# Counting the edges of a graph in windows of twelve nodes: how much of the old counts each window reads back

## The reference, cut to what matters

```python
def _sage_mean(x, src, dst, W_self, W_neigh, b, n_nodes):
    deg = jax.ops.segment_sum(jnp.ones_like(dst, dtype=x.dtype), dst, num_segments=n_nodes)
    agg = jax.ops.segment_sum(x[src], dst, num_segments=n_nodes)
    agg = agg / jnp.maximum(deg, 1.0)[:, None]
    return x @ W_self + agg @ W_neigh + b

h = jax.nn.relu(_sage_mean(x, src, dst, W_self1, W_neigh1, b1, n))
h = _sage_mean(h, src, dst, W_self2, W_neigh2, b2, n)
# ... then a layer with an MLP on every edge, and two more that sum over the same edges
```

## Time and profile before

| | us |
|---|---|
| median of 3 runs | 1679.42 (1676.05 to 1679.87) |
| the profiled execution | 1675.27 |
| its span, first to last instruction | 1673.1 |
| counting, first L1762 to first L853 | 18.36 to 308.12 |

### The profile page before, as it was taken

How to read it: one execution, slowest core, us unless ns; L and a number is a source line. 1 busy time by engine, 2 the same in 40 slices (tenths; PEclk the granted TensorE clock), 3 DMA queues, 4 the chain that set the end, 5 groups by cost and what they waited for, 6 DMA issues and landing times.

```text
span 1673.1 us, 30324 instructions
## 1 busy us (share of the span) xinstructions
PE 1451.8 (87%) x9336; PEld 1032.7 (62%) x9336; DVE 754.3 (45%) x2856; ACT 667.5 (40%) x1243; POOL 763.0 (46%) x806
## 2 busy tenths in 40 slices
PE   4899999999958777888989988998898889877997
PEld 3556666555556566666766766766666667654554
DVE  8799999513333222333243333333432343345445
ACT  6766666410023333443345334433443344331113
POOL 3000000000027777777777777777777777721000
PEclk9999999999978999999999998999899989988999
DMA  2000000020053333333333333333333333300001
GB/s 69 1 1 1 2 2 1 8 61 1 0 147 95 83 81 81 79 89 84 79 85 87 80 82 84 85 82 81 84 88 79 81 86 83 82 21 1 0 1 39
DMA packets 158120, 95.18 MB, mean 57 GB/s; under 512 B 119959, under 2 KB 143422, under 8 KB 158030
## 3 DMA queue, kind: packets, MB, share of 16 engines
q0 software_dynamic: 25024, 51.25, 12.0%
q1 hardware_dynamic: 133006, 42.78, 10.5%
HBM read 87.44 MB, written 6.52 MB: 56 GB/s over the span
## 4 chain that ended last, share of the span: by engine, by line
PE 31%; POOL 13%; DMA 11%; issue 9%; DVE 5%; ACT 1%; DVEq 1%; SPq 1%; POOLq 0%; ACTq 0%
POOL arena L735 13%; DMA arena<-x_w1a,idx 9%; PE ps L1167 6%; PE ps L1052 6%; PE ps L1061 5%; PE ps L1045 4%; PE ps L1041 3%; PE ps L1033 3%; PE ps L1102 2%; PE ps L1151 1%; DVE arena L2049 1%; DVE idx L2016 1%; DVEq L336 1%; DMA x_w1b<-arena 1%; DVE stats L2063 1%
## 5 line engine op out<-in xcount | busy, mean ns | idle before, releaser
L735 POOL DMA_INDIRECT arena<-x_w1a,idx x780 | 737.7, 946 | 713.3 <-issue 674.2
L1478 ACT ACTIVATE arena<-ps 88x512 f32<-88x512 f32 x196 | 116.2, 593 | 480.3 <-PE ps L1033 470.0
L1061 PEld LDWEIGHTS ps<-arena 128*128 128x128 f32 x1568 | 208.6, 196 | 111.5 <-issue 72.8
L2049 DVE TENSOR_TENSOR arena<-ps,bias_b 128x512 f32<-128x512 f32 x196 | 135.5, 691 | 208.0 <-PE ps L1052 208.0
L2044 DVE TENSOR_TENSOR arena<-win_i,late 128x96 f32<-128x96 f32 x196 | 50.8, 259 | 391.8 <-PE ps L1061 378.8
L1041 PE MATMUL ps<-ident_f,arena 128*128 128x128 f32 x784 | 130.1, 290 | 107.3 <-DMA arena<-x_w1a,idx 106.4
L1052 PE MATMUL ps<-w_c,arena 128*128 128x128 f32 x1568 | 222.6, 288 | 0.0
L1303 ACT ACTIVATE adj<-ps 128x300 f32 x392 | 171.0, 451 | 108.3 <-PE ps L800 103.8
L1045 PE MATMUL ps<-arena 88*128 88x512 f32 x392 | 208.0, 612 | 3.1 <-ACT arena L1478 3.1
L1052 PEld LDWEIGHTS ps<-w_c,arena 128*128 128x128 f32 x1568 | 205.9, 205 | 0.3
L1061 PE MATMUL ps<-arena 128*128 128x24 f32 x1568 | 197.9, 264 | 4.9 <-ACT arena L1488 1.4
(11 more groups left out here) (205 smaller groups left out, 1406.7 us busy)
## 6 DMA issues: line engine op xcount, KB each, us to landing
arena<-in_edge_attr SPq DMA_DIRECT2D x196, 128.0 KB, 2.3
arena<-x_w1a,idx POOLq DMA_INDIRECT x782
arena<-x_w1b SPq DMA_DIRECT2D x196, 12.0 KB
x_spill<-arena SPq DMA_DIRECT2D x1, 1600.0 KB, 8.6
x_w1a<-arena SPq DMA_DIRECT2D x6, 256.0 KB, 2.3
x_w1b<-arena SPq DMA_DIRECT2D x6, 256.0 KB, 2.7
arena<-x_spill SPq DMA_DIRECT2D x6, 256.0 KB, 3.4
out_x<-arena SPq DMA_DIRECT2D x3, 512.0 KB
```

The costliest lines, as they stand in the source:

```text
L735: pool.indirect_dma_start(out=z_e[v][:, j * D:(j + 1) * D], out_offset=None, in_=xa_d[:, :], in_offset=bass.IndirectOffsetOnAxis(ap=idx[:, ...
L1061: last = pe.matmul(ps[:, WIN_BANK[v % 2], 0:WIN], msg[:, j * P:(j + 1) * P], oh_e[v][:, j, :], start=(j == 0), stop=(j == J - 1))
L2049: dve.tensor_tensor(msg.rearrange("p (j d) -> p j d", d=D), bank(5, J), over(bias_b, J), ALU.add).then_inc(m_sum[v], 1)
```

## The change

Three things change, and the output stays the same.

The matmul that adds old counts (L800, now L805) reads only the first node of each window, 25 columns, 3200 elements apart, and adds them into PSUM columns 12 apart. The other eleven nodes of a window were never counted before, and ACT overwrites them. Only for the last block of the first front in each round, where the window can reach into columns that the second front has written, all twelve are added: two counts in each round, 14 of 392.

The tests become exact for this: each destination of a half must lie within the window and not above the next half's first node (`highest`, `above`), and in each round the last window that adds only one node must end before the second front's first node (`seam_a`, `seam_b`).

`c1_combine` takes both columns of ones: one operation gives max(degree, 0) and max(degree, 1) into `degrees_x`, for all 25 tiles; `dinv` of the first 20 tiles is computed in one operation after the last round. So L844 reads 386 columns instead of 385.

```diff
-        half_all = arena[:, 11136:11136 + HALVES].bitcast(I32)
-        rel = arena[:, 11528:12312]
+        half_all = arena[:, 11136:11136 + HALVES + 1].bitcast(I32)
+        rel = arena[:, 11532:12316]
+        highest = arena[:, 12320:12320 + HALVES]
+        above = words(2, 3).bitcast(F32)[:, 0:NB * J]
+        degrees_x = arena[:, 13156:13156 + 2 * NT].rearrange("p (k u) -> p k u", u=2)
...
                 pe.wait_ge(adj_written, 8 * i + q + (2 if all_before else 1))
-                pe.matmul(ps[:, bank, 0:NT * WIN_A], ident_h[:, :], adj[:, :, bass.ds(b, WIN_A)],
+                shared = WIN_A if (i % RI, v) == (RI - 1, 2) else 1
+                window = ps[:, bank, 0:NT * WIN_A].rearrange("p (k w) -> p k w", w=WIN_A)
+                pe.matmul(window[:, :, 0:shared], ident_h[:, :], adj[:, :, bass.ds(b, shared)],
                           start=False, stop=True).then_inc(cnt_ready, 1)
...
-                    last = pe.matmul(ps[:, c1_bank(k), 0:3 * D + 1], adj[:, u, k * P:(k + 1) * P], mov_x[:, u, 0:3 * D + 1],
+                    last = pe.matmul(ps[:, c1_bank(k), 0:MOV], adj[:, u, k * P:(k + 1) * P], mov_x[:, u, :],
...
+            own.add(dve.scalar_tensor_tensor(out=highest, in0=half_all[:, 0:HALVES], scalar=WIN_A - 1.0,
+                                             in1=half_all[:, 1:HALVES + 1], op0=ALU.add, op1=ALU.min))
...
-            own.add(dve.tensor_reduce(off[:, 1:2], rel, mybir.AxisListType.X, ALU.max))
+            own.add(dve.tensor_tensor(above.rearrange("p (h j) -> p h j", j=J // 2),
+                                      raw_dst.rearrange("p (h j) -> p h j", j=J // 2), tops, ALU.subtract))
+            own.wait()
+            own.add(dve.tensor_reduce(off[:, 1:2], above, mybir.AxisListType.X, ALU.max))
+            own.wait()
             own.add(dve.tensor_reduce(off[:, 2:3], rel, mybir.AxisListType.X, ALU.min))
...
-                own.add(dve.tensor_scalar(off[:, 1:2], off[:, 1:2], WIN_A - 1.0, None, ALU.subtract))
+                own.add(dve.tensor_tensor(differences[:, 0:ROUNDS], seam_a, seam_b, ALU.subtract))
+                own.wait()
+                own.add(dve.tensor_reduce(off[0:1, 6:7], differences[:, 0:ROUNDS], mybir.AxisListType.X, ALU.max))
+                own.wait()
+                own.add(dve.tensor_scalar(off[0:1, 6:7], off[0:1, 6:7], float(WIN_A), None, ALU.add))
...
                 dve.wait_ge(c1_ready, k + 1)
+                own.add(dve.tensor_tensor(degrees_x[:, k, :], ps[:, b, 3 * D:MOV], win_i[:, 0:2], ALU.max))
                 if k < LATE_TILE:
-                    own.add(dve.tensor_scalar(inv_deg[:, k:k + 1], ps[:, b, 3 * D:3 * D + 1], 1.0, None, ALU.max))
-                    own.add(dve.tensor_scalar(dinv[:, k:k + 1], ps[:, b, 3 * D:3 * D + 1], 1.0, None, ALU.add))
                     own.wait()
-                    own.add(dve.reciprocal(inv_deg[:, k:k + 1], inv_deg[:, k:k + 1]))
+                    own.add(dve.reciprocal(inv_deg[:, k:k + 1], degrees_x[:, k, 1:2]))
...
             dve.wait_ge(c1_deg, 1)
+            own.add(dve.tensor_scalar(dinv[:, 0:LATE_TILE], degrees_x[:, 0:LATE_TILE, 0], 1.0, None, ALU.add))
```

More of the change, by code:

```diff
@@ L1718, in _ @@
             dve.wait_ge(loads[1], 32)
-            firsts = half_all.rearrange("p (h a) -> p h a", a=1).broadcast_to([P, HALVES, J // 2])
+            firsts = half_all[:, 0:HALVES].rearrange("p (h a) -> p h a", a=1).broadcast_to([P, HALVES, J // 2])
+            tops = highest.rearrange("p (h a) -> p h a", a=1).broadcast_to([P, HALVES, J // 2])
+            own.add(dve.scalar_tensor_tensor(out=highest, in0=half_all[:, 0:HALVES], scalar=WIN_A - 1.0,
+                                             in1=half_all[:, 1:HALVES + 1], op0=ALU.add, op1=ALU.min))
             own.add(dve.tensor_tensor(rel.rearrange("p (h j) -> p h j", j=J // 2),
@@ L1753, in in_bounds @@
                 own.add(dve.tensor_scalar(off[0:1, 9:10], off[0:1, 9:10], float(WIN + WIN_A), None, ALU.add))
+                seam_a = base_a.rearrange("p (r m) -> p r m", m=8 * RI)[:, :, 8 * (RI - 1) + 2]
+                seam_b = base_row[0:1, :].rearrange("p (r m) -> p r m", m=RB)[:, :, FB]
+                own.add(dve.tensor_tensor(differences[:, 0:ROUNDS], seam_a, seam_b, ALU.subtract))
[3 more added lines that the diff above has]
+                own.add(dve.tensor_scalar(off[0:1, 6:7], off[0:1, 6:7], float(WIN_A), None, ALU.add))
                 for c in range(EARLY):
@@ L2524 @@
     half_firsts = counted_dst[::SUB]
+    half_bounds = _np.pad(half_firsts, (0, 1), constant_values=NP)
     units = [2 * unit_block(i, unit(q), i // RI) + q % 4 // 2 for i in range(NB // 4) for q in range(8)]
@@ L2528 @@
         "dst_counted": by_edge(counted_dst),
-        "half_firsts": half_firsts,
+        "half_firsts": half_bounds,
         "unit_firsts": half_firsts[units].reshape(1, -1),
```

## The result

| | before | after |
|---|---|---|
| median of the timed runs, us | 1679.34 (1676.05 to 1679.87, 4 runs) | 1660.24 (1659.2 to 1664.54, 4 runs) |
| ratio | | 0.9902, 95% interval 0.9888 to 0.9916 |
| profiled execution / its span, us | 1675.27 / 1673.1 | 1659.71 / 1657.5 |
| first one-hot (DVE) | 18.36 | 20.30 |
| first stage: from there to the 57th one-hot | 83.36 | 79.67 |

The kernel is 1.0% faster; 1662 was forecast. The counting ends 13.2 us earlier. The other 2.3 us of the profiled difference lie behind it, where no edit is.

What follows compares the result with a forecast made beforehand. Rounds 1 and 2: neither PE nor DVE full; rounds 3 to 7: PE bound, DVE right behind. Terms -7.0 -6.5 -1.4 +0.1 -2.8 +1.6 +0.5 = -15.5 gave 1659.8 from 1675.27, 1663.9 from the median; forecast 1662, range 1652 to 1672.

Steps and rivals of the forecast that it cites:

- first stage: Rounds 1 and 2, with work on x: shorter L800 cuts DVE's waits for PE, -7.0 us, bounds 0 and -15.8.
- prologue: Before the first count: DVE's added operations and waits cost +1.6 us, bounds 0 (if an idle time absorbs them) and +1.9.
- second stage: Rounds 3 to 7: DVE becomes the bound, its waits for PE go, -6.5 us; other DVE edits -1.4, +0.1, +0.5.
- end of the rounds: From DVE's last block to L853: PE follows closely, one block is left, about 2.0 us; -2.8, bounds 0 and -3.3.
- L805's place on PE: In each of 378 counts, the 25-column matmul takes 0.05 us on PE, saving 0.11 a count.
- the strides: Rival in L805: strided access costs more than the columns saved; slower by 5 us at 0.168; chance 0.04.
- the window's cost: Rival in L805: windows cost, not columns, so it takes as long as L800; 1679 to 1681 us; chance 0.10.
- ACT holds the stage: Rival in rounds 1 and 2: ACT's loop limits the gain to 2 us; 1667 to 1670 us; chance 0.17.
- all waits go: Rival in rounds 1 and 2: DVE is bound from the first count, -15.8 instead of -7.0; 1653 us; chance 0.10.
- The combine: In c1_combine one two-column operation replaces two; 18 of 20 count at 0.08 us, -1.4, bounds -2.7 and 0.
- small case: Granted clock before L853: a single 3.4 us drop to 1.2 GHz costs at most 1.7 us; called likelier, no chance given.
- large case: Rival: some 40% of rounds 1 and 2 at 1.2 GHz makes the kernel slower by 5 us; 1680 to 1700; chance 0.04.

Runs made afterwards that it cites:

- the split burst: Kernel after with x's own product behind the 4th count and neighbour product behind the 7th, ACT's copies moved accordingly: 1658.66 us, ratio 0.9896.
- the short matmul alone: Kernel before with only the 25-column matmul (300 at the seam), tests, c1_combine and 385 columns unchanged: 1659.3 us, ratio 0.9894.
- the half window: Kernel after with six nodes added instead of one (150 columns, 300 at the seam): 1665.21 us, ratio 0.9923.
- ACT's copies twice: Kernel after with ACT copying each of x's neighbour parts twice, one after the other: 1673.93 us in one run.
- the clearing: Kernel after with DVE clearing three tiles of adj instead of five, ACT and GpSimd the others: 1661.45 us, ratio 0.9905.
- both kernels of the last section: Kernel after with x's products apart, DVE clearing three tiles, tests in round 1: 1656.1 us, ratio 0.9883; the same with bias on GpSimd: 1651.76, 0.9859.
- the rest alone: Kernel after with all 300 columns added again in every count, keeping exact tests, new c1_combine and 386 columns: 1678.27 us, ratio 1.0008.

## Why the prediction was right, and where a size was off

| term at deg | forecast | measured |
|---|---|---|
| prologue | +1.6 | +1.94 |
| first stage | -7.0 | -3.7 |
| second stage (-6.5 -1.4 +0.1 +0.5) | -7.3 | -9.9 |
| end of the rounds | -2.8 | -1.6 |
| sum | -15.5 | -13.2 |

**L805's place on PE: right.** 0.05 was taken, with a break-even at 0.168 for the strides. The trace shows 25 to 29 ns in the second stage, near the row of one column in the earlier trace rows, and up to 39 ns at some places of the first. L800 took 0.148 us on the mean of the second stage; with the 20 ns that the matmul behind L805 loses, PE saves 0.10 us a count, for 0.11 forecast. The rivals of the window's cost and of the strides fall: neither the reads 6400 bytes apart nor the writes of every twelfth word made the matmul longer than one of a single column. "SBUF — State Buffer", section "Door 1: The DMA port swizzle", in the Trainium skill, would have made both patterns slow. A matmul this short can't settle that, since 25 columns in one run would be hidden below the 25 ns as well (385 columns take 0.162 us, so 25 would take 0.011). The experiment with 150 columns and the full windows can: for the reads the trace agrees with the page (150 columns take 64 ns where each run lies within 16 bytes, up to 98 where it does not), for the writes it does not (the 64 ns have gaps in PSUM too, and are 63 by the columns). The last section has the details. "TensorE: Matmul & The Clock Gate", section "Back-to-back issue gap", has a floor of about 25 ns, which the trace bears out.

**First stage: the mis-sized term, 3.7 for 7.0.** The step that failed is "PE is four blocks behind in all of them, so all it gains reaches DVE". That was true of the piece before the change, and the change itself ended it. DVE's timeline after, over one chunk of x and the next:

```profile
61.87 0.43 DVE L1780 TENSOR_TENSOR arena<-late 128x512 bf16<-128x512 bf16 x1 [1.52 <-PE ps L798]
63.05 0.42 DVE L1780 TENSOR_TENSOR arena<-late 128x512 bf16<-128x512 bf16 x1
...
64.55 0.43 DVE L1780 TENSOR_TENSOR arena<-late 128x512 bf16<-128x512 bf16 x1 [0.25 <-PE ps L798]
...
67.19 0.43 DVE L1780 TENSOR_TENSOR arena<-late 128x512 bf16<-128x512 bf16 x1 [0.21 <-PE ps L798]
...
73.08 0.43 DVE L1780 TENSOR_TENSOR arena<-late 128x512 bf16<-128x512 bf16 x1 [1.13 <-PE ps L798]
```

The waits at six bursts, in order, were 1.56, 1.51, 2.34, 1.57, 1.56 and 1.41 us before and 1.39, 1.63, 2.18, 1.52, 1.13 and 1.26 after: 9.95 and 9.11 in all. It was mostly the small waits between that shrank. Between bursts PE now catches up with DVE and then waits, for ACT above all (6.0 us for 3.4). Of the 9.0 us by which PE's busy time fell, 5.3 became idle time of PE and 3.7 reached the stage. DVE's lead of four buffers still does not last through a burst. The gain lay between "all that PE gains" (-7.0) and the rival in which ACT holds the stage (-2), and far from the one in which all waits go. Doubled work on ACT and on PE showed that both are in the chain, and the split burst that the layout of bursts and copies costs; which of the two engines holds how much was not separated.

**Second stage: the mechanism right, the size short by 2.6.** DVE became the bound, as forecast: no wait left, 99% busy, 37.97 us a round. The step that was off is that DVE's waits of 6.9 us were all there was to gain. The idle time shown before an L1762 starts at the end of the instruction before it, but a next block may start about 0.08 us before that end, since DVE's operations overlap. The rows above show it: from 63.05 to 64.55 is 1.50 us, 0.33 more than a block's 1.17, and the bracket says 0.25. The view of waits also leaves out the shortest: it counts 16 of 21. Taken from start to start, the 21 blocks of the kernel before that waited began 9.2 us late in all, and in the kernel after none does. The combine was worth 0.065 and not 0.08, by its period of 1.24 and 1.175 us, 1.2 us for 18. The tests in round 3 take 3.82 us on DVE for 3.45, +0.4 for +0.5 forecast. These come to -10.0, and -9.9 was measured.

**End of the rounds: half.** "What is left after DVE is one block" gave 2.0 us and measured 3.2. The step that was off is the one block of two counts. PE counts two blocks in turn, a half of each, so that at least three counts follow DVE's last block; and PE was one count further behind, since the last counts have two L849 each and last 0.63 us, 1.26 a block, while a block of DVE takes 1.17. When DVE was done at 291.68, PE had the last four counts before it, two of them with the seam's 300 columns. Their first and last:

```profile
291.70 0.42 PE L798 MATMUL ps<-arena 128*128 128x300 bf16 x2
...
293.84 0.42 PE L798 MATMUL ps<-arena 128*128 128x300 bf16 x2
```

**Prologue: right.** With all 300 columns and the new tests, where DVE did not wait for the DMA, the first one-hot came at 19.97: +1.61 for +1.6 forecast. The profiled execution after adds 0.3 of that wait. The doubt about a fixed time of day is settled: the idle 1.61 us moved along.

**The clock: right for this execution, and not the end of it.** The granted clock stayed at 1.00 in the counting of the kernel after. But in six of the ten experiments with a shorter L805 it fell to 0.50 (1.2 GHz) for 3.4 us before deg: the short matmul alone, the half window, ACT's copies twice, the clearing, and both kernels of the last section. With 300 columns, in the kernel before and in the rest alone, it did not. This is round 3 of the kernel with the shared-out clearing, the stretch before the fall and the fall:

```profile
105.00:108.44 3.44, 1.06 (x7) 0.62 (x8) 3.40 (x24) 0.42 (x1) 0.00 (x0) 1.00 0.01 2
108.44:111.85 3.41, 3.41 (x18) 1.90 (x17) 3.41 (x16) 1.35 (x3) 0.00 (x0) 0.50 0.00 0
```

DVE had run its tests from 101.9 to 105.7, and PE, no longer four blocks behind, had run out of one-hots. In all six cases PE was busy for 1.1 to 1.9 us of the 3.4 before the fall. Yet in the kernel after it was busy for 0.8 us from 106.4 to 109.8, and the clock stayed. The price is small: round 3 takes 41.42 us here for 40.79, near 0.6, where the prediction allowed up to 1.7 for a single fall. So its small case is real and its large case never came. The three other timed runs of the kernel after have no trace, so whether they had such a stretch stays open.

Behind deg the clock fell too, but the earlier trace rows don't repeat. In the kernel before it fell 2.8 us behind deg, as the one-column matmuls ended, and again 16.5 us behind deg. In the kernel after it stayed at 1.00 behind the one-column matmuls and fell once, 15.0 us behind deg. First the stretch of after, then the second one of before:

```profile
309.90:313.30 3.40, 3.40 (x13) 1.61 (x11) 2.03 (x4) 2.27 (x4) 0.00 (x0) 0.50 0.00 0
```

```profile
324.60:328.00 3.40, 3.40 (x12) 1.65 (x11) 0.25 (x1) 0.56 (x2) 0.00 (x0) 0.50 0.00 0
```

From deg to the first product of the second aggregate took 29.86 us before and 28.30 after. That is 1.6 of the 2.3 us behind deg. I don't count them to the change: in the profiled executions of the eleven experiments, which change nothing behind deg against one or the other kernel, that part took 1363.6 to 1368.1 us, and before it was 1365.0. The time came out near the forecast by some luck. In the counting, the forecast gave the first stage 3.3 us and the end 1.2 too much, and the second stage 2.6 too little, which made up for part of it; and the part behind deg, where no edit is, happened to fill the gap of 2.3 that was left (13.2 for 15.5).

## What to carry to other kernels

When a faster engine makes another one the bound, the gain is that engine's distance from its undisturbed pace, read from starts and not from the idle time shown; half of the saving may do as well as all of it. A retiming of one piece holds only as long as the lag that it assumes: after the change, retime it from the new state, and ask whether the lead in buffers lasts through the longest burst; laying a burst and its copies out over more time may give what removing work does not. Edits on the engine that is not the bound are worth nothing alone and full price once the first edit has moved the bound, so look for them next.

## What the runs showed of the hardware that was not expected

- A matmul of 25 bf16 columns, read 6400 bytes apart and written to every twelfth word of PSUM, holds PE for 25 to 29 ns at the full clock ahead of an L849 (up to 39 ahead of an L798), as one of a single column does; the one behind it takes some 20 ns more (0.163 to 0.183 for an L849, 0.127 to 0.146 for an L798).
- The place of the full window of 300 columns, in runs of twelve nodes, goes with where its first node lies: 0.127 us when its number modulo 8 is 0, 2 or 4, 0.147 at 1 and 3, 0.162 to 0.168 at 5 to 7. By 0.162 for the 385 columns of an L844 it would be 0.126. The 0.15 and 0.17 of the earlier trace rows are this. The half windows, in runs of six nodes, split by the same number: 64 ns at 0 to 2, 82 to 87 at 4 to 6, 98 at 3 and 7 (medians; 63 by the columns). Eight nodes are 16 bytes. The times are lowest where a run of six lies within one stretch of 16 bytes, and highest where a single node falls into another one; a run of twelve takes longest where it touches three. So the reads' alignment sets the shift, as far as times sorted by node can show it.
- The half windows are written in runs of six words, twelve apart, and take 64 ns for 63 where the reads are aligned: for this pattern the gaps in PSUM cost nothing that shows.
- In six of the eleven profiled executions of kernels with a shorter L805 the granted clock fell to 0.50 for 3.4 us before deg, PE having been busy for 1.1 to 1.9 of the 3.4 us before; in neither of the two with 300 columns did it. In one place PE was busy for 0.8 of 3.4 us, and it stayed at 1.00.
